# Interaction network on one core: VectorE splits x1 one group earlier and sums it one group later, and GpSimd issues four of quad 2's moves

## The chip, the core and the metric

One core of a Trainium2 chip runs the kernel. The metric is the device time of one execution in microseconds. The kernel before takes 678.15 us (median of 3 runs, 677.34 to 679.1).

## The reference

39 embedding rows of 16 numbers are looked up for each of 512 samples. Three interaction layers follow, each with 128 output maps, and a small dense network behind them:

```python
def _cin_layer(X0, Xi, W, b):
    Wr = W.reshape(H, F0_, Fi)
    return jnp.einsum('hjk,bjd,bkd->bhd', Wr, X0, Xi) + b[None, :, None]
# X0: 512 x 39 x 16 embeddings; Xi = X0, then the output of the layer before; H = 128
# every layer's output is summed over its 16 columns and kept
h = relu([sums of the 3 layers, dense_ctx] @ W_top1 + b_top1); h = relu(h @ W_top2 + b_top2); y = h @ W_top3
```

The output is one number for each sample.

## The kernel before

**Tiles and quads.** The 512 samples are cut into 64 tiles of 8 samples (128 columns: 8 samples times 16). Four tiles make a quad, so there are 16 quads, 0 to 15. T counts the tiles, ti = T % 4 is the tile's place in its quad.

**Layer 1** (the second of the three) is the bulk of the work and is done tile by tile. TensorE multiplies x1, the output of the first layer, with the weights in 10 groups g = 0 to 9 of four blocks of 128 columns (group 8 has three): `layer1`, lines 1151 to 1153, three matmuls a group, since x1 and the weights are each held as a high part and a low rest. The results lie in five banks of PSUM, group g in bank g % 5, so group g waits until the group five before it has been read. ScalarE reads groups 0, 1, 3, 4, 6, 7 and 9 (line 725), VectorE groups 2, 5 and 8 (lines 937 and 939). The text calls them VectorE's third, sixth and ninth group. GpSimd adds up pairs of what ScalarE made (`add_groups`, line 526, twice a tile; the second one waits for ScalarE's group 4). VectorE's `reduce_early` (line 947) stands between its groups 5 and 8 and waits for ScalarE's group 6 and for both additions of GpSimd, `reduce_late` (line 955) is done at the start of the next tile.

**Layer 0** makes x1 for the quad that comes next. For each quad GpSimd multiplies seven chunks (`multiply`, line 521; in quad 0 VectorE multiplies three quarters of them, `multiply_rest`, line 915), and TensorE sums them into one PSUM bank, `ps_x1` (`layer0`, line 1065; in quad 0 `sum_rest`, line 1136). The places of the chunks among the groups of layer 1 are written out by hand. While quad q >= 3 runs, chunk 0 of quad q + 1 is summed behind group 2 of the quad's first tile, and the last chunk, called LAST (number 6), behind group 2 of its fourth tile:

```python
SUMMED_AFTER = {(0, 2): 0, (0, 8): 1, (1, 1): 2, (1, 8): 3, (2, 5): 4, (3, 0): 5, (3, 2): LAST}
```

In quads 0 and 1 chunk 0 stands behind group 9 of the second tile, in quad 2 behind group 4 of the first. `ps_x1` is one bank, so chunk 0 has to wait until the x1 before it has been read from there:

```python
if c == 0:
    wait(pe, x1_lo_made, q)
    wait(pe, r1_made, q)
```

**Reading x1.** Three instructions read `ps_x1` in the fourth tile of a quad: ScalarE's `keep_x1` (line 653) makes the high part, VectorE's `split_x1` (line 855) the low rest, and waits for `keep_x1`; VectorE's `sum_x1` (line 860) sums over the 16 columns and signals `r1_made`. In quads 0 and 1 (`FREE_QUADS = 2`) the order on VectorE is: group 2, split, group 5, reduce_early, group 8, sum. In quads 2 to 14 it is: group 2, group 5, split, sum, reduce_early, group 8. ScalarE's `keep_x1` stands behind group 3 in quads 0 and 1 and behind group 4 later.

**Start of quad 0.** Tile 0 works on a quarter of x1 that is made ahead. The other three quarters are made during tile 0. VectorE's order is: group 2, chunks 3 and 4, group 5, chunks 5 and LAST, `spread` (line 848), reduce_early, `split_rest_x1` (line 920), sum_x1, group 8. TensorE sums chunks 5 and LAST behind group 7, then turns the rows of quad 1 (`turn_rows`, line 1028, waits for `spread`). Tile 1 waits for the low part.

**SyncE's queue and the last chunk.** SyncE issues the moves for each quad in a fixed order: shared rows (line 364), windows (line 387), the operands of the last chunk (`load_runs`, lines 374 and 375, four moves into `left` and four into `bz`, 20 KB each), and `lay_out` of the quad after (line 357, 32 moves in general, 16 in the part that is seen here). In quad 2 `load_runs` stands behind `lay_out(3)`. GpSimd gathers table rows (line 493) between its products. In tiles 4 to 7 it makes quad 2's chunks 0, 1, 2, gathers, chunks 3, 4, 5, two copies (lines 505 and 507), two gathers, and chunk LAST.

**Others.** Tiles 8 to 27 carry some extra work (the weights of layer 2 are turned): among the fourth tiles of quads, those of quads 2 to 6.

Of the kernel before, what the change touches and what calls it, by code (L numbers as in the profile page):

```python
# [35 lines left out]
RUN = 10  # L36
# [67 lines left out]
    return multiplied(q) if q == 3 else list(range(CHUNKS))  # L104


FIRST_SUMMED_AFTER = {2: [0], 3: [1], 4: [2], 5: [3], 6: [4], 7: [5, 6]}

SECOND_REGROUPED_AFTER = 3
NEXT_TURNED_AFTER, NEXT_KEPT_AFTER = [(0, 7), (0, 1)], [(0, 7), (0, 3)]  # L110
# [68 lines left out]
def build(nc, dense_ctx, ids, bases, table, W_top1, b_top1, W_top2, b_top2, W_top3, W0, b0, W1, b1, W2, b2, out):  # L179
# [8 lines left out]
    with ExitStack() as ctx:  # L188
# [117 lines left out]
        first_window = [None] + [sem(f"first_window_{c}") for c in range(1, LAST)]  # L306
        z_made, z_used = sem("z_made"), sem("z_used")
        runs_ld = [sem("runs_ld_0"), sem("runs_ld_1")]
        first_cut = [sem("first_cut_0"), sem("first_cut_1")]
        first_runs = sem("first_runs")  # L310
        z_hi_made, z_lo_made, z_stacked = sem("z_hi_made"), sem("z_lo_made"), sem("z_stacked")
# [37 lines left out]
        def _(sp):  # L349
# [16 lines left out]
            def load_runs(q, landed):  # L366

                if q - 1 >= STACKED_FROM:
                    sp.wait_ge(z_lo_made, q - STACKED_FROM)
                else:  # L370
                    sp.wait_ge(z_used, CHUNKS * (q - 1) + summed(q - 1).index(LAST) + 1)
                for n, (l, r) in enumerate(RUNS):
                    at = slice(RUN * n, RUN * (n + 1))
                    sp.dma_start(left[at, :], x0[l:l + RUN, q % 2, :]).then_inc(landed, 16)
                    sp.dma_start(bz[at, LAST, :], x0[r:r + RUN, q % 2, :]).then_inc(landed, 16)

            def stack(q):
# [99 lines left out]
        def _(pool):  # L477
# [31 lines left out]
            def multiply(q, c):  # L509
                if c == 0:  # L510
                    wait(pool, shared[q % 2], 16 * (SPC + 1) * ((q + 1) // 2))
                    wait(pool, z_used, CHUNKS * (q - 1) + 1)
                if c == 1:
                    wait(pool, first_cut[q % 2], 16 * len(window_parts(1)) * ((q + 1) // 2))
                if c == 2:
                    wait(pool, cut[q % 2], 16 * WINDOWS * ((q + 1) // 2))
                if c == LAST:
                    wait(pool, runs_ld[q % 2], 16 * 2 * len(RUNS) * ((q + 1) // 2))
                r = chunk_rows(c)
                window = bz[0:r, c, :] if c else x0[0:r, q % 2, :]  # L520
                nc.gpsimd.tensor_tensor(bz[0:r, c, :], window, left if c == LAST else xa[0:r, :], ALU.mult).then_inc(z_made, 1)  # L521
# [65 lines left out]
            multiply(2, 0)  # L587
            gather_behind(3, 9)
            multiply(2, 1)
            multiply(2, 2)  # L590
            make_index(4)
            for g in range(3):
# [37 lines left out]
        def _(act):  # L630
# [105 lines left out]
            for T in range(TILES):  # L736
# [3 lines left out]
                for g in ACT_GROUPS:  # L740
                    scale(T, g)
                    if (q, ti, g) == (1, 0, 4):
                        nc.scalar.copy(w0_stack[0:LEFT_ROWS, :], w0t[0:LEFT_ROWS, LAST, :]).then_inc(w0_hi_made, 1)
                    if STACKED_FROM <= q + 1 < QUADS and (ti, g) == SPLIT_LAST_AFTER:
                        split_last(q + 1)
                    if g == 6 and ti == 1 and q + 1 < QUADS:
                        keep_xt(q + 1)
                    if g == (3 if q < FREE_QUADS else 4) and ti == 3 and q + 1 < QUADS:
                        keep_x1(q + 1)
                    if (T, g) == (0, 7):  # L750
                        keep_rest_x1()
                    if (T, g) == (0, SECOND_REGROUPED_AFTER):
                        act.wait_ge(gathered[1], 16 * GATHERS)
                        for f in range(FPG // 2):
                            ins = regroup(nc.scalar.copy, 1, f)
                        ins.then_inc(regrouped_act, 1)
                    if q < FREE_QUADS and (ti, g) == NEXT_KEPT_AFTER[q]:
                        keep_x0(q + 1)
                    if FREE_QUADS - 1 <= q < QUADS - 2 and (ti, g) == (KEPT_AFTER if q >= FREE_QUADS else THIRD_KEPT_AFTER):
                        keep_x0(q + 2)  # L760
                    if g == 7 and T > 0:
                        keep_g(T - 1)
                    if g == 6 and T in W2_TURNED_IN:
                        n = W2_TURNED_IN[T]
                        act.wait_ge(w2_turned, n + 1)
                        nc.scalar.copy(w2_home(False, n).bitcast(F32R),
                                       ps_tr[:].rearrange("p (r c) -> p r c", c=HALF)).then_inc(w2_hi_made, 1)
# [20 lines left out]
        def _(dve):  # L788
# [173 lines left out]
            for T in range(TILES):  # L962
# [6 lines left out]
                if T == 0:  # L969
                    multiply_rest(3)  # L970
                    multiply_rest(4)
                if ti == 3 and q < FREE_QUADS:
                    split_x1(q + 1)
                scale_and_sum(T, DVE_GROUPS[1])
                if T == 0:
                    multiply_rest(5)
                    multiply_rest(6)
                    spread(0)
                if ti == 3 and FREE_QUADS <= q < QUADS - 1:
                    split_x1(q + 1)  # L980
                    sum_x1(q + 1)
                reduce_early(T)
                if T == 0:
                    split_rest_x1()
                    sum_x1(0)
                scale_and_sum(T, DVE_GROUPS[2])
                if ti == 3 and q < FREE_QUADS:
                    sum_x1(q + 1)
                if T == QT:
                    dve.wait_ge(w0_hi_made, 1)  # L990
# [276 lines left out]
```

## Time and profile before

| | |
|---|---|
| median of 3 runs | 678.15 us (677.34 to 679.1) |
| profiled execution | 677.4 us, span of the core 674.6 us |
| mean granted clock | 0.995 |
| TensorE busy | 653.3 us, 97% |
| ScalarE / VectorE / GpSimd busy | 572.2 / 517.9 / 455.4 us |

The profile follows one execution. The span runs from the first to the last instruction, and 2.8 us lie around it. TensorE is busy nearly all the time, so what matters is where TensorE waits. Its matmuls overlap, and the end of each is modelled: a stall is read from the distance between starts. In a stretch without a wait three matmuls of 512 columns start 0.23 to 0.24 us apart, and a group takes 0.70 us.

### The profile page before, as it was taken

Reading aid. Unit: us, or ns where it says so; the run is one execution under the profiler, and the core shown is the slowest. Engines: PE = TensorE matmul, PEld = TensorE weight load, DVE = VectorE, ACT = ScalarE, POOL = GpSimd, SP = SyncE. Lnnn points to the kernel's source line nnn. Section 1 sums busy time; section 2 is a strip of 40 time slices with the busy share of each in tenths; the row PEclk is TensorE's granted clock in tenths of the full one; section 3 lists DMA queues with packets and bytes.
Section 4 is the critical chain, followed back from the end, with each engine's and each line's share of the span. In section 5 each row is a group of like instructions: output and inputs, shape, how many; then the busy total and the mean of one; then the engine's idle time right before and its main releaser. Section 6 shows DMA issues by size and latency. Waiting matters only on the chain. (4 is left out here: it accounts for less than half of the span.)

```text
span 674.6 us, 10670 instructions
## 1 busy us (share of the span) xinstructions
PE 653.3 (97%) x2692; PEld 480.0 (71%) x2692; DVE 517.9 (77%) x1015; ACT 572.2 (85%) x2010; POOL 455.4 (68%) x443
## 2 busy tenths in 40 slices
PE   4889998999999999999999999999999999999998
PEld 4666766777777777777777777777777777776683
DVE  6578785678787878797878878788878797888780
ACT  3667976889898989898999989898989898999672
POOL 6748657777787878787887878787878655333000
PEclk9989998999999999999999999999999999999999
DMA  7222134223433425142421313131323121204300
GB/s 213 77 69 46 32 71 106 45 68 75 113 98 66 146 21 185 13 142 41 122 60 42 78 25 95 15 105 16 100 19 99 13 82 31 89 2 162 142 0 0
DMA packets 111155, 49.35 MB, mean 73 GB/s; under 512 B 82837, under 2 KB 95001, under 8 KB 111094
## 3 DMA queue, kind: packets, MB, share of 16 engines
q1 hardware_dynamic: 105120, 46.23, 26.1%
q0 software_dynamic: 5120, 1.29, 2.1%
q10 hardware_dynamic: 854, 1.16, 0.6%
q8 instruction: 21, 0.34, 0.2%
q14 instruction: 40, 0.33, 0.2%
HBM read 13.81 MB, written 5.24 MB: 28 GB/s over the span
## 5 line engine op out<-in xcount | busy, mean ns | idle before, releaser
L725 ACT ACTIVATE prod<-ps_y,xt 128x128 f32<-128x128 f32 x1792 | 494.7, 426 | 61.6 <-PE ps_y L1153 57.3
L1151 PE MATMUL ps_y<-w_hi,x_hi 128*128 128x512 f32 (+1 forms) x640 | 304.0, 475 | 2.3 <-issue 1.1
L1152 PE MATMUL ps_y<-w_lo,x_hi 128*128 128x512 f32 (+1 forms) x640 | 249.9, 391 | 0.0
L1153 PE MATMUL ps_y<-w_hi,x_lo 128*128 128x512 f32 (+1 forms) x640 | 249.9, 390 | 0.0
L526 POOL TENSOR_TENSOR prod<-prod 128x512 f32<-128x512 f32 x118 | 152.4, 1292 | 80.9 <-ACT prod L725 78.5
L939 DVE SCALAR_TENSOR_TENSOR prod<-ps_y,xt,prod 128x128 f32<-128x128 f32 x576 | 162.9, 341 | 30.4 <-PE ps_y L1153 30.1
L493 POOL DMA_INDIRECT rows<-in_table,index x160 | 155.2, 970 | 45.0 <-issue 31.2
L947 DVE TENSOR_REDUCE prod<-prod 128x128 f32<-128x1536 f32 (+1 forms) x64 | 117.5, 1835 | 57.3 <-ACT prod L725 43.3
L1151 PEld LDWEIGHTS ps_y<-w_hi,x_hi 128*128 128x128 f32 x640 | 120.8, 189 | 56.2 <-issue 20.5
L1152 PEld LDWEIGHTS ps_y<-w_lo,x_hi 128*128 128x128 f32 x640 | 121.2, 189 | 43.4 <-issue 20.4
L1153 PEld LDWEIGHTS ps_y<-w_hi,x_lo 128*128 128x128 f32 x640 | 121.0, 189 | 26.2
L521 POOL TENSOR_TENSOR room<-room 128x512 f32<-128x512 f32 (+2 forms) x90 | 115.8, 1294 | 7.7 <-DMA room<-room 7.5
L955 DVE TENSOR_REDUCE x<-prod 128x128 f32<-128x1536 f32 x64 | 111.8, 1747 | 6.0 <-ACT prod L725 2.7
L1065 PE MATMUL ps_x<-room,w0t 117*128 117x512 f32 (+5 forms) x186 | 96.1, 597 | 3.1 <-POOL room L521 3.1
L1168 PE MATMUL ps_g<-bd,x 128*128 128x320 f32 x128 | 45.4, 435 | 0.0
L1065 PEld LDWEIGHTS ps_x<-room,w0t 117*128 117x128 f32 (+5 forms) x186 | 33.9, 189 | 11.7 <-POOL room L521 5.2
L937 DVE TENSOR_SCALAR prod<-ps_y,xt 128x128 f32<-128x128 f32 x128 | 38.4, 341 | 0.7 <-PE ps_y L1153 0.6
L734 ACT COPY g_all<-ps_g 128x320 f32<-128x320 f32 x64 | 31.1, 485 | 3.4 <-PE ps_g L1168 3.4
L1168 PEld LDWEIGHTS ps_g<-bd,x 128*128 128x128 f32 x128 | 23.4, 190 | 7.6 <-DVE x L955 2.9
L773 ACT CAST g_hi<-g_all 128x512 fp32r<-128x512 f32 x39 | 23.9, 621 | 4.5 <-PE ps_y L1214 2.3
L505 POOL COPY emb_room<-emb_room 128x312 f32<-128x312 f32 x15 | 7.2, 477 | 24.9 <-DMA emb_room<-rows 24.9
L848 DVE TENSOR_TENSOR bd<-ps_tr,mask 128x1248 f32<-128x1248 f32 x16 | 23.1, 1443 | 0.0
(138 smaller groups left out, 367.1 us busy)
## 6 DMA issues: line engine op xcount, KB each, us to landing
room<-room SPq DMA_DIRECT2D x75, 234.0 KB
room<-room SPq DMA_DIRECT2D x45, 78.0 KB
emb_room<-rows SPq DMA_DIRECT2D x168, 5.0 KB
rows<-in_table,index POOLq DMA_INDIRECT x160
w_hi_dram<-g_all SPq DMA_DIRECT2D x5, 512.0 KB
w_lo_dram<-g_all SPq DMA_DIRECT2D x5, 512.0 KB
g_all<-in_L_rec_W SPq DMA_DIRECT2D x9, 256.0 KB, 6.1
g_all<-in_L_rec_W SPq DMA_DIRECT2D x4, 512.0 KB, 4.2
```

The lines of the kernel that those rows point to most:

```text
L493: pool.indirect_dma_start(out=rows[0:n, q % 2, g, :], out_offset=None, in_=table, in_offset=bass.IndirectOffsetOnAxis(ap=index[0:n, q % 2, ...
L521: nc.gpsimd.tensor_tensor(bz[0:r, c, :], window, left if c == LAST else xa[0:r, :], ALU.mult).then_inc(z_made, 1)
L526: nc.gpsimd.tensor_tensor(prod[:, SLOT[a]:SLOT[a] + 2], prod[:, SLOT[a]:SLOT[a] + 2], prod[:, SLOT[b]:SLOT[b] + 2], ALU.add).then_inc(pool ...
L725: ins = nc.scalar.activation(prod[:, SLOT[k] + m // 2, :, m % 2], ps_y[:, g % YBANKS, m * H:(m + 1) * H], ACT.Copy, scale=xt[:, q % 2, ti, ...
L939: ins = nc.vector.scalar_tensor_tensor(out=a, in0=y, scalar=x, in1=a, op0=ALU.mult, op1=ALU.add)
L947: nc.vector.tensor_reduce(prod[:, BIASED, :, 0], prod[:, EARLY if adds(T) else EARLY_FIRST].rearrange("p n h l -> p h n l"), AX_XY, ALU.ad ...
L955: nc.vector.tensor_reduce(x2[:, T % 2, :], prod[:, LATE[T % 2]].rearrange("p n h l -> p h n l"), AX_XY, ALU.add).then_inc(reduced, 1)
L1065: nc.tensor.matmul(ps_x1[:], w, z, start=c == 0, stop=c == summed(q)[-1]).then_inc(z_used, 1)
L1151: nc.tensor.matmul(y, hi, w1_hi[:, cols], start=True, stop=False)
L1152: nc.tensor.matmul(y, hi, w1_lo[:, cols], start=False, stop=False)
L1153: nc.tensor.matmul(y, lo, w1_hi[:, cols], start=False, stop=True).then_inc(y_made, 1)
L1168: nc.tensor.matmul(ps_g[:, 0:(F + 1) * TB], x2[:, T % 2, :], bd[:, T // QT % 2, T % QT].rearrange("p j b -> p (j b)"), start=True, stop=Tr ...
```

## The change

In every quad that makes a next x1 (0 to 14) VectorE's order in the fourth tile becomes: group 2, split_x1, group 5, reduce_early, group 8, sum_x1. ScalarE's `keep_x1` stands behind group 3 in all of them. In tile 0 the last chunk is multiplied behind reduce_early, x1 is split and summed behind group 8, TensorE sums the last chunk behind group 9 and ScalarE makes the high part behind its group 9. SyncE no longer issues the four moves into `left` for quad 2. GpSimd issues them behind chunk 1 of quad 2, and its last product of quad 2 waits for them by a semaphore of their own.

```diff
-FIRST_SUMMED_AFTER = {2: [0], 3: [1], 4: [2], 5: [3], 6: [4], 7: [5, 6]}
+FIRST_SUMMED_AFTER = {2: [0], 3: [1], 4: [2], 5: [3], 6: [4], 7: [5], 9: [LAST]}
...
+        left_ld = sem("left_ld")
...
-                    sp.dma_start(left[at, :], x0[l:l + RUN, q % 2, :]).then_inc(landed, 16)
+                    if q != 2:
+                        sp.dma_start(left[at, :], x0[l:l + RUN, q % 2, :]).then_inc(landed, 16)
                     sp.dma_start(bz[at, LAST, :], x0[r:r + RUN, q % 2, :]).then_inc(landed, 16)
...
                 if c == LAST:
-                    wait(pool, runs_ld[q % 2], 16 * 2 * len(RUNS) * ((q + 1) // 2))
+                    if q == 2:
+                        pool.wait_ge(left_ld, 16 * len(RUNS))
+
+                    wait(pool, runs_ld[q % 2], 16 * len(RUNS) * (2 * ((q + 1) // 2) - (q % 2 == 0)))
...
             multiply(2, 1)
+
+            pool.wait_ge(x0_made, 3)
+            pool.wait_ge(z_made, CHUNKS * 2)
+            for n, (l, r) in enumerate(RUNS):
+                pool.dma_start(left[RUN * n:RUN * (n + 1), :], x0[l:l + RUN, 0, :]).then_inc(left_ld, 16)
             multiply(2, 2)
...
-                    if g == (3 if q < FREE_QUADS else 4) and ti == 3 and q + 1 < QUADS:
+                    if g == 3 and ti == 3 and q + 1 < QUADS:
                         keep_x1(q + 1)
-                    if (T, g) == (0, 7):
+                    if (T, g) == (0, 9):
                         keep_rest_x1()
...
-                if ti == 3 and q < FREE_QUADS:
+                if ti == 3 and q + 1 < QUADS:
                     split_x1(q + 1)
                 scale_and_sum(T, DVE_GROUPS[1])
                 if T == 0:
                     multiply_rest(5)
-                    multiply_rest(6)
                     spread(0)
-                if ti == 3 and FREE_QUADS <= q < QUADS - 1:
-                    split_x1(q + 1)
-                    sum_x1(q + 1)
                 reduce_early(T)
+                if T == 0:
+                    multiply_rest(LAST)
+                scale_and_sum(T, DVE_GROUPS[2])
                 if T == 0:
                     split_rest_x1()
                     sum_x1(0)
-                scale_and_sum(T, DVE_GROUPS[2])
-                if ti == 3 and q < FREE_QUADS:
+                if ti == 3 and q + 1 < QUADS:
                     sum_x1(q + 1)
```

## Rows read from the trace of the kernel before

**Rows 1.** Page, part 1: busy us, share of the span, instructions.
```profile
PE 653.3 (97%) x2692; PEld 480.0 (71%) x2692; DVE 517.9 (77%) x1015; ACT 572.2 (85%) x2010; POOL 455.4 (68%) x443
```

**Rows 2.** Waits of PE: who, for whom, us in total, times, longest.
```profile
PE ps_x L1065 <- POOL room L521: 3.1, 4, 2.2
```

**Rows 3.** Timeline of PE, tile 7: start, us, instruction, count, idle before.
```profile
108.96 1.12 PE L1065 MATMUL ps_x<-room,w0t 40*128 40x512 f32 x2 [2.18 <-POOL room L521]
```

**Rows 4.** Timeline of GpSimd and of SyncE's queue, tiles 5 to 7.
```profile
85.93 1.32 POOL L521 TENSOR_TENSOR room<-room 127x512 f32<-127x512 f32 x1
93.52 1.29 POOL L521 TENSOR_TENSOR room<-room 126x512 f32<-126x512 f32 x1 [6.27 <-DMA room<-room]
107.65 1.25 POOL L521 TENSOR_TENSOR room<-room,g_hi 40x512 f32<-40x512 f32 x1 [2.22 <-DMA room<-room]
...
100.00 0.82 SPq L374 DMA_DIRECT2D g_hi<-room  x1
105.48 0.72 SPq L375 DMA_DIRECT2D room<-room  x1
```

**Rows 5.** Page, part 5, GpSimd's gathers: count, busy us, mean ns, idle before.
```profile
L493 POOL DMA_INDIRECT rows<-in_table,index x160 | 155.2, 970 | 45.0 <-issue 31.2
```

**Rows 6.** Stretches: width, PE, PEld, DVE, ACT, POOL busy (count), PE clock, DMA, GB/s.
```profile
39.50:42.90 3.40, 2.90 (x10) 2.55 (x10) 3.40 (x3) 1.16 (x2) 0.57 (x1) 0.50 0.00 0
111.20:114.60 3.40, 3.40 (x10) 2.61 (x9) 1.76 (x5) 2.65 (x9) 3.01 (x4) 0.50 0.42 125
114.70:118.00 3.30, 3.30 (x16) 2.72 (x15) 2.17 (x3) 3.12 (x12) 2.98 (x4) 1.00 0.53 168
```

**Rows 7.** Timeline of PE and of DVE, tile 0.
```profile
38.54 0.91 PE L1136 MATMUL ps_x<-room,w0t 40*128 40x384 f32 x2 [1.66 <-DVE room L915]
43.16 0.50 PE L1151 MATMUL ps_y<-w_hi,x_hi 128*128 128x512 f32 x1
...
37.94 0.55 DVE L915 TENSOR_TENSOR room<-room,g_hi 40x384 f32<-40x384 f32 x1 [2.78 <-DMA room<-room]
38.41 1.44 DVE L848 TENSOR_TENSOR bd<-ps_tr,mask 128x1248 f32<-128x1248 f32 x1
39.78 2.80 DVE L947 TENSOR_REDUCE prod<-prod 128x128 f32<-128x2560 f32 x1
42.51 0.60 DVE L920 SCALAR_TENSOR_TENSOR x_lo<-ps_x,columns,x_hi 128x384 fp32r<-128x384 f32 x1
```

**Rows 8.** Timeline of ACT, tile 0.
```profile
39.49 0.58 ACT L708 ACTIVATE x_hi<-ps_x,columns 128x384 fp32r<-128x384 f32 x1 [2.07 <-PE ps_x L1136]
```

**Rows 9.** Timeline of PE, DVE, ACT, POOL, tile 47 into 48.
```profile
484.05 1.02 PE L1065 MATMUL ps_x<-room,w0t 128*128 128x512 f32 x2
...
481.11 0.68 DVE L860 TENSOR_REDUCE r<-ps_x 128x32 f32<-128x512 f32 x1
481.70 1.74 DVE L947 TENSOR_REDUCE prod<-prod 128x128 f32<-128x1536 f32 x1
483.37 0.86 DVE L939 SCALAR_TENSOR_TENSOR prod<-ps_y,xt,prod 128x128 f32<-128x128 f32 x3
...
479.66 0.74 ACT L653 ACTIVATE x_hi<-ps_x,columns 128x512 fp32r<-128x512 f32 x1
...
480.11 1.31 POOL L526 TENSOR_TENSOR prod<-prod 128x512 f32<-128x512 f32 x1
```

**Rows 10.** The same places, tile 19 into 20: PE, then DVE.
```profile
230.27 1.02 PE L1065 MATMUL ps_x<-room,w0t 128*128 128x512 f32 x2
...
229.18 0.86 DVE L939 SCALAR_TENSOR_TENSOR prod<-ps_y,xt,prod 128x128 f32<-128x128 f32 x3
```

**Rows 11.** The same places, tile 43 into 44: PE, then POOL.
```profile
447.73 1.02 PE L1065 MATMUL ps_x<-room,w0t 128*128 128x512 f32 x2
448.90 0.50 PE L1151 MATMUL ps_y<-w_hi,x_hi 128*128 128x512 f32 x1 [0.15 <-DVE prod L939]
...
444.91 1.32 POOL L526 TENSOR_TENSOR prod<-prod 128x512 f32<-128x512 f32 x1
```

## The prediction, written before the changed kernel ran

> **What bounds the kernel now.** I read the page's part 1 first: PE is busy 97% of the span, the next engine 85% [rows 1]. TensorE is the bound, and a gain or a loss has to show as a wait of TensorE or as a change of its clock. So the second view is the list of PE's waits. Only two entries of it belong to the change: the sums of layer 0 waiting for GpSimd's products, 3.1 us in all, of which one wait is 2.2 us [rows 2], and the sum in tile 0 waiting for VectorE, 1.7 us [rows 7]. The third view is the timeline at these two places, the fourth the granted clock of stretches around them, and the last the timelines of all engines at the end of a quad, since the change reorders work there in every quad.
>
> **Quad 2's last chunk.** TensorE stands 2.18 us in tile 7 until GpSimd has multiplied the last chunk [rows 3]. GpSimd itself stood 2.22 us before this product, from 105.43 to 107.65, for the moves of the operands [rows 4]. SyncE issued those eight moves one after another, from 100.00 to 106.20, so 0.78 us each, and the data were there 1.45 us after the last issue [rows 4]. With four of them gone the last of SyncE's four is issued at about 103.1 and has landed at about 104.6, before GpSimd is ready at 105.43. The product then ends at 106.7 and not at 108.9. TensorE is ready for the chunk at about 106.6, so nearly all of its wait goes: 2.1 us.
>
> The four moves that GpSimd takes over stand behind chunk 1's product, which ends at 87.25, and GpSimd then stands until 93.52 for the windows [rows 4]. A direct move issued by GpSimd isn't in the trace. Its nearest row is an indirect one of GpSimd, 0.97 us on average [rows 5]; from below the nearest is SyncE's 0.72 us [rows 4]. Four cost 2.9 to 3.9 us and up to 5 us with the gaps between gathers, and the idle stretch of 6.27 us covers all of it. If that cover were gone, chunks 2 to LAST would be late by the whole of it. The two waits put ahead of them (x0_made, z_made) are for things that earlier instructions of GpSimd already needed: nothing. The four moves run beside the window moves that end that idle stretch. Each carries 10 rows, a window 117 to 127, and there are eight window moves; I take 0.1 us, between 0 and 0.4.
>
> The Trainium skill, page "DMA: Bandwidth & Descriptors", section "Issuing engines are not separate DMA queues", speaks against this part: moves from any engine run on the same 16 DMA engines, and a second issuer saves only the sequencer's time, "which is usually small relative to the DMA itself". Here the trace differs: the sequencer's 6.2 us stand against 1.45 us from the last issue to the data [rows 4]. By the page's rule this part would bring nothing; that is the third rival below.
>
> **The clock behind it.** From 111.2 to 114.6 the granted clock is 0.50, that is 1.2 GHz, right behind this wait, and TensorE starts 10 matmuls there, against 16 in the next 3.3 us at full clock [rows 6]. The lost part is half of 3.4 us, 1.7 us. The only other stretch at 0.50 within these tiles follows the other long wait, in tile 0 [rows 6, 7]. With the wait gone I expect the second drop to go as well: 1.7 us. TensorE then reaches tile 8's group 3 earlier than GpSimd's additions and VectorE's group 8 of tile 7 allow, by about 0.4 us, since GpSimd gains only 2.2 us. Sum for quad 2: 2.1 + 1.7 - 0.4 + 0.1 of cost = 3.3 gained, bounds 1.6 (the drop stays) to 3.9.
>
> **Tile 0.** Now VectorE waits 2.78 us for the last chunk's operands, from 35.16 on, and spread (1.44) and reduce_early (2.80) stand behind it [rows 7]. In the new order spread runs at once and ends at 36.5, reduce_early ends at 39.3, the last product (0.55) at 39.75. TensorE meanwhile turns the rows and does groups 8 and 9, which end at about 38.8; at present they come only behind the last chunk. It sums the last chunk at 39.8, that is 1.2 us later than now (38.54). ScalarE starts the high part 0.95 us after that sum's start [rows 7, 8]: 40.75, done at 41.33; VectorE has done group 8 by then and splits until 41.95 (0.60). Tile 1 starts at about 42.0 and not at 43.16 [rows 7]: 1.1 us gained. sum_x1, 0.68 us behind it, is next needed a tile later: nothing.
> **The clock in tile 1** counts against this. Now the drop from 39.5 on [rows 6] costs next to nothing, as tile 1 has to wait for the split at 43.11 anyhow. In the new order TensorE waits 1.0 us and then 1.4 us within 3.3 us, and a drop that follows falls on tile 1, where TensorE has no wait: 1.7 us. I take it that it comes. Tile 0: +0.6 us, bounds -1.1 and +0.7.
>
> **The end of every quad from 2 on.** This decides. In tile 47 the present order is split, sum_x1 481.11 (0.68), reduce_early 481.70 (1.74), group 8 from 483.37 to 484.23, and TensorE starts chunk 0 of the quad after next at 484.05 [rows 9]. That chunk waits for `r1_made`, which sum_x1 signals, and this was done at 481.79: a margin of 2.3 us. In the new order sum_x1 stands behind group 8. It can't end before about 484.8, and the chunk waits for it, at the head of TensorE's queue, with group 3 of the next tile and all behind it.
>
> Does reduce_early come earlier, now that split and sum no longer stand right before it? It waits for ScalarE's group 6, which is not moved by the swap (keep_x1 and group 4 change places), and for GpSimd's second addition, which waits for group 4. ScalarE's keep_x1 takes 0.57 us of its time (0.74 [rows 9], of which the next instruction overlaps some 0.17), so group 4 is later by that: it ends at about 480.4 and not at 479.8, the addition runs from 480.5 to 481.8 and not from 480.11 [rows 9]. reduce_early starts at about 481.88, 0.2 us later than now. Group 8 ends at 484.4, sum_x1 at 485.0, chunk 0 starts at 485.05: TensorE loses 1.0 us.
> - Seven quad ends are of this kind (tiles 31, 35, ... 55). In five of them, as tile 43, GpSimd is late: its second addition starts 2.8 us ahead of TensorE's chunk 0 (444.91, 447.73) where in tile 47 it is 3.9 us, and group 3 of the next tile already waits for VectorE's group 8, starting 1.17 us behind chunk 0 and not some 0.46 [rows 9, 11]. If GpSimd stays late the loss there is 1.05 us. If a longer quad lets it catch up (its lateness comes from waiting for the lay_out moves), it is 0.5 us in the three latest and 0.9 us in the others. I take that it catches up: 3 x 0.5 + 2 x 0.9 + 2 x 1.0 = 5.3.
> - Five quad ends (tiles 11, 15, 19, 23, 27) have a turn of four blocks behind group 4, so TensorE comes to chunk 0 later against VectorE: at 230.27, 0.23 behind the end of group 8, and not 0.18 ahead of it [rows 9, 10]. 5 x 0.58 = 2.9.
>
> Sum 8.2 us. From above, with GpSimd as late as now, 10.6. From below, if GpSimd's addition never held reduce_early, so that ScalarE's group 6 set it: 3.9. I take 8.2, as group 4 and the addition behind it are rows with little play. The earlier split brings nothing: TensorE has no wait on x_lo after tile 1. Group 5 comes 1.1 us later at most, and its bank is next needed 0.7 us behind its new end, in a tile of the first kind. The last two quad ends make no chunk 0 behind them or stand in quads 0 and 1, where the order is already the new one.
>
> **Sum.** 677.4 - 3.3 + 0.6 + 8.2 = 682.9 us for the profiled execution. That execution is 0.75 us under the median of the three runs, so the same sum gives 683.6 at the median. I predict 683.3.
>
> **The rivals.**
> - *The clock drops at the quad ends too.* A wait of 1 us is new in 12 places. For it: both long waits of the trace are followed by 0.50 [rows 6]. Against: those were 1.7 and 2.2 us long, and two stretches of 3.4 us at 0.50 are all that the mean clock of 0.995 leaves room for, so no shorter wait brought one. Each drop costs 1.7 us; four of them give 690, all twelve 704. The Trainium skill ("TensorE: Matmul & The Clock Gate", section "HAM oscillation") tells of a loop where this comes back at "every single K-tile". Chance 0.12.
> - *Faster: VectorE is done in time.* If sum_x1 ended before TensorE comes to chunk 0, only the gains at quads 0 and 2 would stay: 678.15 - 3.3 - 1.1 = 673.7. It decides at a loss of 0.37 us a quad end, under which the gains outweigh it; VectorE's group 8 would have to end some 0.4 us earlier than now. For it: VectorE is idle 23% of the span [rows 1]. Against: of the two releases of reduce_early one doesn't move and one moves later. With the lower bound of 3.9 and no drop in tile 1 the time is 677.7. Chance of this side 0.08.
> - *Quad 2's chunk comes no earlier.* GpSimd's own moves land late or cost more than the idle stretch, and the wait of 2.2 us and the drop stay: 683.3 + 3.3 = 686.6. Chance 0.15.
> - *The chunk 0 wait is there, but the net is nothing* (loss near its lower end, both gains full): 678. Chance 0.05.
>
> The forecast has 0.60. Its own range is 680.5 to 686. The whole range, 679 to 689, takes in the third rival and a few clock drops. A difference of 0.3% is 2.0 us, about what a measurement can tell here. Faster 0.08 is the second rival; same 0.08 is the fourth and 0.03 from the forecast's lower edge; the rest, 0.84, is slower.
>
> **What would show it.** In the changed profile: PE's waits list gets an entry of layer 0 (now line 1065) released by VectorE's sum_x1, 12 times, around 0.6 to 1.0 us each. GpSimd's last product of quad 2 starts within 0.1 us of its gather's end, and PE's wait for it is under 0.3 us. Four moves on GpSimd's queue lie in the stretch where it waited 6.27 us. Tile 1 starts about 1 us earlier. Quads 8 to 14 last about 0.8 us longer each. The prediction is wrong if TensorE starts chunk 0 where it does now, or if the granted clock shows more than two stretches at 0.50.

## The result and the profile after

The changed kernel takes 683.45 us (median of 6 runs, 682.24 to 687.47) against 678.19 us for the kernel before (6 runs on the same chip): the ratio is 1.0085, interval 1.0063 to 1.0107. The profiled execution took 685.1 us, span 683.0 us. The forecast, 683.3 us, and its sign came out. That the number is so near is in part luck: in the profiled execution the term for tile 0 was 2.1 us too high and the one for the quad ends 2.0 us too low, and the two errors cancelled.

First the page of after, part 1 (busy us, share, instructions):

```profile
PE 653.3 (96%) x2692; PEld 478.7 (70%) x2692; DVE 519.0 (76%) x1015; ACT 573.5 (84%) x2010; POOL 458.1 (67%) x447
```

Beside [rows 1] no engine has more work to speak of; GpSimd has four instructions more. TensorE's 653.3 us are the same, so the 8.3 us by which the span grew are waits. The waits of PE (for whom, who ended them, us in total, times, longest):

```profile
PE ps_x L1073 <- issue: 8.8, 12, 1.0
PE ps_y L1159 <- DVE x_lo L930: 1.3, 1, 1.3
PE ps_y L1159 <- DVE prod L949: 1.2, 4, 0.5
PE ps_x L1144 <- DVE room L925: 1.1, 1, 1.1
PE ps_x L1073 <- POOL room L526: 0.5, 2, 0.3
```

Line 1073 is `layer0`, 1065 before. The first entry is new: 12 waits, 8.8 us. The list counts 8.8 us, where the starts of the matmuls give a loss of 10.2 us (the table below): a wait in the list begins only at the modelled end of the matmul before it. The fifth entry is what is left of [rows 2], where it was 3.1 us. The second and fourth are tile 0. The third stood at 1.0 us in 4 waits before.

**Where the time went.** I took the distance from the first matmul of each tile to that of the next in both profiled executions, and summed it by quad:

| stretch | after minus before, us | forecast |
|---|---|---|
| start of the span to tile 0 | +2.93 | 0 |
| quad 0 (all of it in tile 0: 16.36 to 14.84) | -1.52 | +0.6 |
| quad 1 (tile 7: 13.36 to 9.64) | -3.84 | -3.7 |
| quad 2 (tile 8: 9.96 to 10.48) | +0.52 | +0.4 |
| quads 3 to 14: .75 .71 .72 .71 .77 1.14 .91 1.00 .83 .98 .59 1.13 | +10.24 | +8.2 |
| quad 15 | -0.02 | 0 |
| sum | +8.3 | +5.5 |

**The quad end.** Timelines of PE, ACT, DVE and POOL in tile 47 and the start of 48 (start, us, instruction, idle before). This execution is later as a whole: TensorE starts group 3 of tile 47 at 482.33 here and at 476.69 in before, and times are compared counted from there:

```profile
490.75 1.10 PE L1073 MATMUL ps_x<-room,w0t 128*128 128x512 f32 x2 [0.89 <-issue]
491.28 0.79 PE L1159 MATMUL ps_y<-w_hi,x_hi 128*128 128x512 f32 x1
...
484.31 0.71 ACT L663 ACTIVATE x_hi<-ps_x,columns 128x512 fp32r<-128x512 f32 x1
...
485.05 0.75 DVE L865 SCALAR_TENSOR_TENSOR x_lo<-ps_x,columns,x_hi 128x512 fp32r<-128x512 f32 x1 [1.04 <-ACT x_hi L663]
487.52 1.75 DVE L957 TENSOR_REDUCE prod<-prod 128x128 f32<-128x1536 f32 x1 [0.69 <-ACT prod L735]
489.19 0.86 DVE L949 SCALAR_TENSOR_TENSOR prod<-ps_y,xt,prod 128x128 f32<-128x128 f32 x3
489.96 0.68 DVE L870 TENSOR_REDUCE r<-ps_x 128x32 f32<-128x512 f32 x1
...
486.13 1.30 POOL L531 TENSOR_TENSOR prod<-prod 128x512 f32<-128x512 f32 x1 [0.40 <-ACT prod L735]
```

`sum_x1` (line 870) runs from 489.96 to 490.64, and chunk 0 starts at 490.75, 0.1 us behind its end. Before, the same sum ended at 481.79 and the chunk started at 484.05 [rows 9]: a margin of 2.3 us has become a wait of 0.89. VectorE works through reduce_early, group 8 and the sum without a gap, and was idle 0.69 and 1.04 us just before. The list of waits names the releaser "issue" and not the sum; that it is the sum is read from the 0.1 us between the two, which is the same at all twelve quad ends (tiles 11, 15, ... 55), and shown by the experiments.

**Quad 2's last chunk.** Tile 7: PE, then POOL, then SyncE's queue.

```profile
107.69 0.39 PE L1161 MATMUL ps_y<-w_hi,x_lo 128*128 128x512 f32 x1
108.11 1.12 PE L1073 MATMUL ps_x<-room,w0t 40*128 40x512 f32 x2
...
88.58 2.14 POOL L599 DMA_DIRECT2D g_hi<-room  x4
94.37 1.30 POOL L526 TENSOR_TENSOR room<-room 126x512 f32<-126x512 f32 x1 [3.65 <-DMA room<-room]
106.74 1.31 POOL L526 TENSOR_TENSOR room<-room,g_hi 40x512 f32<-40x512 f32 x1
...
102.01 3.17 SPq L377 DMA_DIRECT2D room<-room  x4
```

The 2.22 us of GpSimd and the 2.18 us of TensorE [rows 3, 4] are gone. SyncE issues four moves (102.01 to 105.18) and not eight. GpSimd's four took 2.14 us, 0.54 each, inside the stretch in which it had waited 6.27 us.

**The clock and tile 0.** Stretches (width, PE, PEld, DVE, ACT, POOL busy, clock, DMA, GB/s), then PE and DVE of tile 0:

```profile
112.00:116.00 4.00, 4.00 (x19) 3.26 (x19) 3.31 (x6) 4.00 (x17) 3.64 (x4) 1.00 0.44 139
27.00:44.00 17.00, 14.33 (x66) 10.22 (x65) 11.56 (x25) 11.49 (x42) 9.52 (x18) 1.00 0.27 76
```
```profile
42.34 0.91 PE L1144 MATMUL ps_x<-room,w0t 40*128 40x384 f32 x2 [1.13 <-DVE room L925]
44.57 0.50 PE L1159 MATMUL ps_y<-w_hi,x_hi 128*128 128x512 f32 x1 [1.32 <-DVE x_lo L930]
...
37.65 1.45 DVE L858 TENSOR_TENSOR bd<-ps_tr,mask 128x1248 f32<-128x1248 f32 x1
39.02 2.81 DVE L957 TENSOR_REDUCE prod<-prod 128x128 f32<-128x2560 f32 x1
41.74 0.54 DVE L925 TENSOR_TENSOR room<-room,g_hi 40x384 f32<-40x384 f32 x1
43.90 0.62 DVE L930 SCALAR_TENSOR_TENSOR x_lo<-ps_x,columns,x_hi 128x384 fp32r<-128x384 f32 x1 [0.84 <-ACT x_hi L718]
```

Both stretches at half clock of [rows 6] are gone. The order in tile 0 is the forecast one, with waits of 1.13 and 1.32 us, and here no drop followed them.

### The profile page after: what moved, and what is told of

It is laid out like the page before. It is cut to its first block and busy times, and to the rows that moved or that the text cites. A ratio compares the mean times of both kernels' runs of the same rounds, so it can differ in the third digit from the quotient of the medians.

```text
span 683.0 us, 10672 instructions
## 1 busy us (share of the span) xinstructions
PE 653.3 (96%) x2692; PEld 478.7 (70%) x2692; DVE 519.0 (76%) x1015; ACT 573.5 (84%) x2010; POOL 458.1 (67%) x447
## 5 line engine op out<-in xcount | busy, mean ns | idle before, releaser
L495 POOL DMA_INDIRECT rows<-in_table,index x160 | 157.4, 984 | 43.8 <-issue 28.5
L865 DVE SCALAR_TENSOR_TENSOR x_lo<-ps_x,columns,x_hi 128x512 fp32r<-128x512 f32 x15 | 11.3, 751 | 18.7 <-ACT x_hi L663 16.6
```

The costliest lines, as they stand in the source:

```text
L495: pool.indirect_dma_start(out=rows[0:n, q % 2, g, :], out_offset=None, in_=table, in_offset=bass.IndirectOffsetOnAxis(ap=index[0:n, q % 2, ...
```

## The experiments

The chips of the three batches differ: the kernel before has a median of 683.4, 683.6 and 677.9 us on them, and the profiled executions differ mostly in the stretch ahead of tile 0 (the kernel with GpSimd's moves alone starts tile 0 at 33.3 us on the second chip and at 26.3 us on the third). Ratios are therefore each to the kernel before on the same chip, and where a run is said to be some us longer or shorter, that is its ratio times this median, unless medians are named. An expected time is compared by its ratio to 678.2 us. "Quads 3 to 14" is the sum of the table above, against the profiled execution of before.

### What in the quad end costs the time

Only the sum goes back ahead of reduce_early; the early split and keep_x1 stay:

```diff
+                if ti == 3 and FREE_QUADS <= q < QUADS - 1:
+                    sum_x1(q + 1)
                 reduce_early(T)
 ...
-                if ti == 3 and q + 1 < QUADS:
+                if ti == 3 and q < FREE_QUADS:
                     sum_x1(q + 1)
```

> The changed kernel, with sum_x1 put back ahead of reduce_early from quad 2 on; the earlier split and ScalarE's earlier keep_x1 stay. Theory (the sum behind group 8 holds TensorE's chunk 0 of the next quad, 12 times some 0.85 us, 10.2 us in all in the profile after): the waits for sum_x1 go and the time falls from 683.4 to about 673. Rival 1 (the swap of keep_x1 and group 4, which makes GpSimd's second addition and reduce_early 0.2 us later, costs a good part): it stays above 676. Rival 2 (the earlier split itself brings something): it comes out more than 1 us under the kernel with the whole quad end undone.

Measured: 682.3 us, ratio 0.997 (0.9941 to 0.9999). The waits of chunk 0 are gone; quads 3 to 14 take 1.7 us more than before, mostly in small stalls of tiles 31 to 43, where after has 10.2. The time is not the expected one: 673 us would be a ratio of 0.992.

The whole quad end of before put back into after:

```diff
-                    if g == 3 and ti == 3 and q + 1 < QUADS:
+                    if g == (3 if q < FREE_QUADS else 4) and ti == 3 and q + 1 < QUADS:
 ...
+                if ti == 3 and FREE_QUADS <= q < QUADS - 1:
+                    split_x1(q + 1)
+                    sum_x1(q + 1)
                 reduce_early(T)
 ...
```

> The changed kernel with the whole quad end as before from quad 2 on (group 5, split, sum, reduce_early, group 8; keep_x1 behind ScalarE's group 4); the parts in tile 0 and at quad 2's last chunk stay. Theory: these two parts alone bring 1.1 to 1.5 us and 3.8 us less 0.4 us, against the kernel before: 673.0 to 674.0. If they bring nothing in the median, 678.

Measured: 682.9 us, ratio 0.9973 (0.9937 to 1.0009); quads 3 to 14 +1.3, with one stall of 1.5 in tile 35. The two kernels differ by 0.6 us, well inside either interval: that split and keep_x1 stand earlier is worth nothing that shows in the medians. What costs is where the sum stands. This run too is short of its expectation, 0.992 to 0.994, which was for the two other parts alone. As the quad ends of the two kernels differ and their times do not, the shortfall lies outside the quad ends; the new order in tile 0 turns out below to be worth less than the expectation took.

The stall in tile 35 is a wait for the low part, which the list of TensorE's waits of this run shows so:

```profile
PE ps_y L1162 <- DVE x_lo L865: 1.3, 1, 1.3
```

VectorE had stood for 2.42 us ahead of its group 5, and so ahead of the split. The profile names TensorE as what it waited for, but by their records the matmuls of that group end 2.6 us before VectorE reads them. The ends are modelled, so a late end and a late signal can't be told apart. Such a wait for the split of a quad end stands in four of the eight profiled executions with the split behind group 5 (0.6, 0.6, 1.3 and, in four waits, 2.9 us) and in none of the six with the split ahead of it. So the earlier split may guard TensorE when VectorE's group 5 is late. No run tests that by itself.

The release later, or its user later? Chunk 0 is summed behind group 4 and not behind group 2:

```diff
-SUMMED_AFTER = {(0, 2): 0, (0, 8): 1, (1, 1): 2, (1, 8): 3, (2, 5): 4, (3, 0): 5, (3, 2): LAST}
+SUMMED_AFTER = {(0, 4): 0, (0, 8): 1, (1, 1): 2, (1, 8): 3, (2, 5): 4, (3, 0): 5, (3, 2): LAST}
```

> The changed kernel, all parts kept, but chunk 0 of the next quad is summed behind group 4 and not group 2 of a quad's first tile, from quad 3 on. Theory (TensorE waits at chunk 0 for the sum alone): chunk 0 then comes 1.4 us later, 0.8 us behind the end of sum_x1, no wait is left and the time is 673 to 674. Rival (VectorE's queue as a whole is late at this place, so that the wait moves to groups 3 or 7): above 677.

Measured: 684.2 us, ratio 1.0017 (0.999 to 1.0044), where 0.993 was expected of a chunk that waits for nothing and the kernel with the sum back reached 0.997. Waits of PE and the same place in tile 48:

```profile
PE ps_y L1159 <- DVE prod L949: 3.3, 11, 0.5
...
491.13 0.50 PE L1159 MATMUL ps_y<-w_hi,x_hi 128*128 128x512 f32 x1 [0.25 <-DVE prod L949]
492.64 1.02 PE L1073 MATMUL ps_x<-room,w0t 128*128 128x512 f32 x2
```

The wait for the sum is gone. In its place group 3 of the next tile waits for VectorE's group 8, whose bank it takes: that group ends 7.72 us behind the start of TensorE's group 3, and group 3 of the next tile starts at 7.77. The waits are 3.3 us in the list (1.0 us of them, 4 times, stood there before too), and quads 3 to 14 take 3.4 us more than before, a third of after's loss. In before, chunk 0 stands at this place and is 0.46 us of work that covers the same group 8 (7.53 there). The chunk can't leave its place for nothing.

The margin tested from the other side, by a second sum in each quad end:

```diff
                     sum_x1(q + 1)
+                    if q >= FREE_QUADS:
+                        nc.vector.tensor_reduce(r1[:, QB * (q + 1):QB * (q + 2)].rearrange("p (t b) -> p t b", b=TB),
+                                                ps_x1[:].rearrange("p (t d b) -> p t b d", d=D, b=TB), AX_X,
+                                                ALU.add).then_inc(summed_once, 1)
+                        dve.wait_ge(summed_once, q - 1)
```

> The changed kernel, with the sum over x1's columns done twice in a row at each quad end from quad 2 on (the same numbers are written twice). One more sum costs VectorE 0.68 us and a short wait for the first. Theory (sum_x1 stands on TensorE's path at 12 quad ends): 12 times 0.65 to 0.75 us are added, 691 to 693. Rival (there is play behind it): under 687.

Measured: 701.7 us, ratio 1.0248 (1.0193 to 1.0303).

```profile
PE ps_x L1079 <- issue: 18.0, 12, 1.9
165.04 2.04 PE L1079 MATMUL ps_x<-room,w0t 128*128 128x512 f32 x2 [1.85 <-issue]
```

The same 12 waits are 18.0 us, 0.77 longer each; each of quads 4 to 14 takes 0.62 to 0.76 more than in after, and quads 3 to 14 together 11.3 more. The second sum is paid in full: in after there is no slack left at this place. Tile 12 alone takes 13.55 us and not 10.9 as its like in the other quads. Its wait, the second line, is the longest of the twelve, and the granted clock is at half from 164.9 to 168.3, from about the end of this wait. The other eleven, of 1.2 to 1.6 us, have no half clock behind them. By the ratios this kernel is 11.1 us over after, where 7.6 to 9.6 was expected; 2.6 us of it is what tile 12 has over its like.

### The parts alone

Only the quad ends, put into before (three places: keep_x1 behind group 3, split behind group 2, sum behind group 8):

> The kernel before with the new quad ends alone (split ahead of group 5, sum behind group 8, keep_x1 behind group 3, from quad 2 on). Theory: 12 waits of chunk 0, 10 us more than the 678.2 of the kernel before, 687.5 to 689. Rival (the parts add up otherwise, GpSimd stays late without the others): 690.

Measured: 694.7 us, ratio 1.0174 (1.0126 to 1.0222), that is +11.9 us.

```profile
PE ps_x L1062 <- issue: 9.4, 12, 1.1
PE ps_x L1062 <- POOL room L521: 3.3, 2, 3.1
```

The first line is the loss (11.2 us over quads 3 to 14); the second holds the wait for quad 2's last chunk, which this kernel keeps; it was 2.2 us in before. Its quads 4 to 14 are those of after within 0.05 us each; the first, quad 3, has 1.75 where after has 0.75. The ratio is that of the rival (690 us), but its reason is not borne out: GpSimd catches up as in after. VectorE at the quad end ahead of it:

```profile
157.73 0.75 DVE L855 SCALAR_TENSOR_TENSOR x_lo<-ps_x,columns,x_hi 128x512 fp32r<-128x512 f32 x1 [2.46 <-ACT x_hi L653]
```

In after the same wait is 1.43 us. The extra 1.0 us begins on ScalarE: it reads group 3 of tile 11 from 2.40 us behind TensorE's start of that group, and in after from 1.35, though the records of the matmuls stand alike. The run with the sum twice has the same delay at the same place. Its cause stays open, as in tile 35 above.

Only GpSimd's four moves, put into before:

```diff
-                    sp.dma_start(left[at, :], x0[l:l + RUN, q % 2, :]).then_inc(landed, 16)
+                    if q != 2:
+                        sp.dma_start(left[at, :], x0[l:l + RUN, q % 2, :]).then_inc(landed, 16)
 ...
+            for n, (l, r) in enumerate(RUNS):
+                pool.dma_start(left[RUN * n:RUN * (n + 1), :], x0[l:l + RUN, 0, :]).then_inc(left_ld, 16)
```

> The kernel before with GpSimd issuing quad 2's four moves into left, and nothing else. Theory (SyncE's queue of issues is what makes the last chunk late): GpSimd's last product of quad 2 starts right behind its gathers, TensorE's wait of 2.2 us goes and the stretch at half clock with it: 678.2 - 3.4 = 674.8. If the half clock comes all the same: 676.3. Rival (the DMA engines are the limit, whoever issues): 678.

Measured: 680.3 us, ratio 0.9949 (0.9922 to 0.9976), that is -3.5 us, as expected (0.995); tile 7 takes 9.64 us.

```profile
92.22 2.15 POOL L599 DMA_DIRECT2D g_hi<-room  x4
98.59 1.30 POOL L526 TENSOR_TENSOR room<-room 126x512 f32<-126x512 f32 x1 [4.22 <-DMA room<-room]
110.63 1.30 POOL L526 TENSOR_TENSOR room<-room,g_hi 40x512 f32<-40x512 f32 x1
```

Is it GpSimd as a second issuer, or that the four moves go out early? Before, with the four moves issued by SyncE ahead of lay_out(3):

```diff
+                if q == 2:
+                    for n, (l, r) in enumerate(RUNS):
+                        sp.dma_start(left[RUN * n:RUN * (n + 1), :], x0[l:l + RUN, 0, :]).then_inc(runs_ld[0], 16)
```

> The kernel before with the same four moves into left still issued by SyncE, but ahead of lay_out(3) and not behind it. Theory (SyncE's issues follow one another without a gap from 78.8 to 106.2 us, so only a second issuer helps): lay_out is 2.9 us later, the four moves into bz still end at 106, GpSimd's last product starts at about 107.6 as now, and the time stays within 0.5 us of 678.2. Rival (what helps is that fewer moves stand behind lay_out, whoever issues them): 674.8 as with GpSimd.

Measured: 682.3 us, ratio 0.9987 (0.9957 to 1.0018): no gain to be told. SyncE's queue, GpSimd, and the waits of PE:

```profile
92.48 3.02 SPq L439 DMA_DIRECT2D g_hi<-room  x4
95.61 10.57 SPq L357 DMA_DIRECT2D emb_room<-rows  x16
106.23 3.15 SPq L376 DMA_DIRECT2D room<-room  x4
...
107.52 0.44 POOL L509 COPY emb_room<-emb_room 128x312 f32<-128x312 f32 x1 [1.81 <-DMA emb_room<-rows]
110.94 1.28 POOL L525 TENSOR_TENSOR room<-room,g_hi 40x512 f32<-40x512 f32 x1 [0.40 <-DMA room<-room]
...
PE ps_tr L1032 <- POOL emb_room L511: 2.2, 1, 2.2
```

The four moves cost SyncE 3.02 us here too, as half of its eight did in before (3.1 of 6.2). Put ahead, they push lay_out back by as much, GpSimd's copy stands 1.81 us for it, and TensorE's 2.2 us stand at turn_rows. Tile 7 is shorter (13.36 to 10.00), with no half clock left in it, and tile 6 longer (13.31 to 14.85). That is 1.8 us gained over both, where GpSimd's moves gain 3.6. So in the trace the rival has half of the gain, and the second issuer the other half. The profiled execution gives it back in quads 3 to 14 (+3.6 us, 2.9 of it in four waits for the low part, told of above), and the median can't tell 1.8 us from none.

Only tile 0's new order, put into before (last chunk behind reduce_early, split behind group 8, summed behind TensorE's group 9):

> The kernel before with the new order in tile 0 alone (last chunk multiplied behind reduce_early, x1 split and summed behind group 8, the last chunk summed behind group 9). Theory A (the two waits of about 1 us do not bring the half clock into tile 1): 1.1 to 1.5 us faster, 676.7 to 677.1. Theory B, the prediction's (half clock falls on tile 1): 0.6 us slower, 678.8.

Measured: 686.0 us, ratio 1.0041 (1.0008 to 1.0074), that is +2.8 us, more than either theory had. Tile 0 takes 14.83 us (16.36 before), tile 1 10.38 us (9.0 in after). Stretches around it:

```profile
45.50:48.90 3.40, 1.27 (x4) 0.29 (x2) 2.56 (x6) 1.73 (x5) 0.87 (x1) 1.00 0.12 25
49.00:52.40 3.40, 3.17 (x8) 2.50 (x9) 2.44 (x3) 1.29 (x5) 0.94 (x1) 0.50 0.36 113
52.50:55.90 3.40, 3.40 (x18) 2.53 (x17) 1.30 (x5) 2.99 (x12) 1.88 (x2) 1.00 0.52 160
```

That is the drop on tile 1 of the forecast: 8 matmuls at 1.2 GHz where the next stretch has 18, behind a stretch in which TensorE was busy 1.27 of 3.40 us. It is not the whole difference. In tile 7 GpSimd waits longer than in before for the last chunk's operands, and TensorE with it:

```profile
115.90 1.25 POOL L521 TENSOR_TENSOR room<-room,g_hi 40x512 f32<-40x512 f32 x1 [3.08 <-DMA room<-room]
```

TensorE stands 3.04 us and not 2.18 there, the half clock behind it lasts 6.8 us and not 3.4, and tile 7 takes 15.79 us for 13.36. The kernel with the quad ends alone, on the same chip, has the longer wait too. The kernel before was not profiled on this chip, so whether the chip or the change makes it longer stays open, and with it how much of the 2.8 us is tile 0's.

### All parts on one chip, and two versions

Four kernels beside 23 runs of before (677.9 us). After itself again:

> The changed kernel itself, beside the next three on one chip, since the chips of the runs so far differ by some 5 us in the time of the kernel before. Theory: it stands to the kernel before as the sum of its parts, the quad ends some 10 us, the moves -3.5 us, tile 0 between -1.5 and +2.8 us: 1.008 to 1.014.

Measured: 684.1 us, ratio 1.0083 (1.0065 to 1.01); quads 3 to 14 +10.2. With the quad end of before, as above:

> The changed kernel with the quad ends as before, on the same chip as the changed kernel. Theory (12 waits of chunk 0 for sum_x1, 0.6 to 1.1 us each): 9 to 10.5 us under the changed kernel, and, as tile 0's new order gains nothing when the prologue is slow, 0 to 3 us under the kernel before.

Measured: 674.3 us, ratio 0.9955 (0.9934 to 0.9976); quads 3 to 14 -0.03, and of the waits of layer 0 only this one is left:

```profile
PE ps_x L1076 <- POOL room L526: 0.8, 2, 0.6
```

The quad end is the one difference between these two kernels, and it is 9.8 us between the medians, 8.7 us by the ratios, 10.2 us over quads 3 to 14 of the traces. GpSimd's moves without the rest:

> The kernel before with GpSimd's four moves alone, on the same chip as the others. Theory: 3.5 us faster than before, 0.995, and faster than every kernel that has the new quad ends or the new tile 0.

Measured: 673.6 us, ratio 0.9943 (0.9924 to 0.9962). And a middle way for tile 0: spread ahead of the last chunk's product, which stays ahead of reduce_early and is summed behind group 8, with the split, the sum and ScalarE's high part of tile 0 where they were, and the quad end of before (against after):

```diff
 ...
                     multiply_rest(5)
                     spread(0)
+                    multiply_rest(LAST)
+                if ti == 3 and FREE_QUADS <= q < QUADS - 1:
+                    split_x1(q + 1)
+                    sum_x1(q + 1)
                 reduce_early(T)
 ...
```

> The kernel before with GpSimd's four moves and a smaller step in tile 0: spread is put ahead of the last chunk's product and TensorE sums the last chunk behind group 8; reduce_early, split and sum stay where they were. VectorE then fills its wait for the operands with spread (1.44 us), and TensorE fills its own with the turn and group 8. Theory (the new order of tile 0 costs since the product stands behind the 2.8 us of reduce_early): tile 0 gets 0.5 to 1.4 us shorter than in the kernel with the moves alone, which is 1.005 times faster than before; this one 0.992 to 0.994. Rival (tile 0 is bound by reduce_early and the split in any order): the same as with the moves alone, 0.995.

Measured: 673.0 us, ratio 0.9936 (0.9914 to 0.9959), the fastest of all, but only 0.5 us under the moves alone; that is not told apart. Its tile 0 takes 14.29 us against 16.60, and its tile 1 10.36 against 9.02, as a half clock now falls on tile 1. VectorE, and then PE's first matmul behind the wait for the low part, there:

```profile
35.98 1.45 DVE L858 TENSOR_TENSOR bd<-ps_tr,mask 128x1248 f32<-128x1248 f32 x1
38.48 0.55 DVE L925 TENSOR_TENSOR room<-room,g_hi 40x384 f32<-40x384 f32 x1 [1.05 <-DMA room<-room]
...
42.34 0.80 PE L1161 MATMUL ps_y<-w_hi,x_hi 128*128 128x512 f32 x1 [1.45 <-DVE x_lo L930]
```

From before to after on this chip, by medians, the steps are: moves -4.3 (677.9 to 673.6), tile 0 +0.7 (to 674.3, inside the noise), quad ends +9.8 (to 684.1). Such steps make +6.2 by construction. Whether the parts add up is told by the runs with each part alone, and they don't quite: +11.9, -3.5 and +2.8 make +11.2, and after stands at +5.6 by its ratio. The intervals, taken together, leave room for some 4.5 us of this difference. The parts were measured on another chip than the whole, and the rest stays open.

## Why the prediction was right, and where it was not

**Quad 2's last chunk: right.** Forecast 3.3 gained, the trace shows 3.32 (quads 1 and 2 together), the runs of this part alone 3.5 and 3.9 by the ratios. The wait, the drop behind it and GpSimd's lag of 0.4 to 0.5 us in tile 8 came as worked out. The cost of GpSimd's moves was taken too high: 2.9 to 3.9 us from the gathers [rows 5], measured 2.14. As the idle stretch covered them either way, nothing followed. The Trainium skill ("DMA: Bandwidth & Descriptors", section "Issuing engines are not separate DMA queues") says that a second issuer saves only the sequencer's time, and that this is usually small. The second half does not hold here. The moved issues were 3.0 to 3.2 us of a queue that was itself the bound, and SyncE issuing them earlier moved 2.2 us of waiting to turn_rows.

**The quad ends: the mechanism right, the size 2.0 us too small.** Of the steps for tile 47, seen from TensorE's group 3 of that tile, the addition of GpSimd (forecast 3.8, measured 3.80), reduce_early (5.19), group 8's end (7.72) and the sum's end (8.31) are all within 0.05 us of the forecast, and chunk 0 starts at 8.42 for 8.35 (8.41 to 8.43 in ten of the twelve, 8.56 in tile 43 and 8.82 in tile 11, where GpSimd's addition is later). That GpSimd catches up was right in four of the five late quad ends; in tile 43 it is still 0.13 us late. The terms that were mis-sized are two. In the clean case I had group 3 start at 8.81, and it starts at 8.95 (7.82 before): the chunk comes 0.07 later and the group 0.53 and not 0.46 behind it, and this is paid in all 12 quads. In the late case I took the loss from the starts of group 3, where it had already waited for group 8 [rows 11]. But that wait had been partly free: when group 3 starts on time, group 4 follows 1.11 us behind (tile 48, 7.82 and 8.93), as the rest of the chunk's work lies between; when it starts late, 0.80 us behind (tile 44, 8.64 and 9.44). A wait ahead of the chunk is paid in full. In after the first tile of quads 8 to 14 takes 10.2 to 10.3 us whatever it took before (9.08 to 9.53). The run with the sum back shows what the sum's place is worth alone: 8.5 of the 10.2 us. Two slips of the recorded text belong here. Its bound from above, 10.6, comes to 10.15 by its own terms (5 x 1.05 + 2 x 1.0 + 2.9). And its sum gives 683.6 at the median, which it lowers to 683.3 without a reason.

**Tile 0: not one number.** In the trace of after the part gained 1.5 us, and no drop fell on tile 1. Of the eight profiled executions with the new order four had a half clock in tile 1 (10.4 to 10.5 us) and four did not; of five with the old order none had it there. So the forecast drop is real and comes in half of the executions; I had taken it as certain. The gain of 1.1 us is not a constant either: with the old order tile 0 is as long as the last chunk's operands take to land. Counted from the start of tile 0 the product begins at 11.14 us in before, 11.38 in one run of the moves alone, 9.73 in the other, 9.26 with the quad ends alone and 8.23 with SyncE's moves ahead, and tile 0 takes 16.36, 16.60, 14.96, 14.49 and 13.45 us. VectorE in tile 0 of the 16.60 us one, and of the 13.45 us one:

```profile
37.71 0.55 DVE L925 TENSOR_TENSOR room<-room,g_hi 40x384 f32<-40x384 f32 x1 [3.03 <-DMA room<-room]
```
```profile
41.48 0.55 DVE L919 TENSOR_TENSOR room<-room,g_hi 40x384 f32<-40x384 f32 x1 [0.22 <-DMA room<-room]
```

The new order puts the product behind reduce_early, at 12.0 us or later, so it never takes less than 14.83, and took 16.4 in the five executions in which a half clock fell into it, 15.74 in one without. Where the operands land late it can win 1.5 us; where they land early it loses. The forecast worked from one execution in which they landed late [rows 7]. The step that failed is that one landing time was taken for all. Tile 0 cost 0.7 us between the medians of the moves alone and the same with the new order, which their intervals don't tell from nothing, and 2.8 us put alone into before, on another chip and with a longer wait in tile 7; the forecast was +0.6.

**Outside the sum** stand the 2.9 us by which the profiled execution of after came later to tile 0, with the same instructions as before there. That execution is 2.2 us over the forecast 682.9: +2.9 there, +2.0 at the quad ends, -2.1 in tile 0, and 0.6 less outside the span. The median is within 0.2 us of 683.3.

**The rivals.** The clock did not drop at the quad ends: after's span has one stretch at half clock, at 22.5 to 25.9, ahead of tile 0. That VectorE is in time is refuted by the 12 waits; that the chunk comes no earlier, by tile 7; that the net is nothing, by 10.2 us lost at the quad ends against 4.8 gained in quads 0 to 2. The sign by which that wait was to be known failed, though the wait came: the forecast wait would be listed as released by VectorE; it is listed as "issue".

**What stays open:** why the stretch ahead of tile 0 lasts 26 to 30 us in the executions of the result and of the last batch and 33 to 35 in the others; what decides whether a half clock follows in tile 1; why VectorE and ScalarE read a group 1 to 2.6 us late at a few quad ends; whether the earlier split guards TensorE then; why the wait in tile 7 is 3.0 us and not 2.2 in two kernels on the second chip; and whether spread ahead of the product is worth its 0.5 us.

## What to carry to other kernels

An instruction that frees a buffer is placed by when its user needs the buffer, not by when the instruction's own input is ready: here a sum of 0.68 us with 2.3 us of margin was put behind 2.6 us of other work, and 12 times TensorE paid up to 1.0 us. When a wait is removed by moving its user, look at what is next late on the same engine. Where one queue issues small moves at 0.8 us each and the data are there 1.5 us after the last, a second issuer helps; another order in the same queue brought half as much in the trace, because it made others in the queue wait, and nothing to be told in the median. And the parts of a change are best measured as steps on one chip: alone, on another one, they made 11.2 us where the whole was 5.6.

## What the runs showed of the hardware

- A direct move of 10 rows of 2 KB took GpSimd 0.54 us to issue, an indirect one 0.97 [rows 5], one of SyncE 0.72 to 0.82 [rows 4].
- A fall of TensorE's clock to 1.2 GHz is not the same from one execution to the next: behind waits of 1.1 and 1.3 us in tile 0 it came in four of eight. The twelve waits at the quad ends of after, five of 0.45 to 0.56 us and seven of 0.9 to 1.0, brought none; with the sum done twice they were 1.2 to 1.9 us, and it came behind the longest alone.
- The kernel before ran 0.8% slower on two chips than on the third. No profile of it was taken there. The kernel with GpSimd's moves alone, profiled on one of the two and on the third, has spans of 678.6 and 671.4 us, and starts tile 0 at 33.3 and 26.3 us.
- At a few quad ends VectorE or ScalarE read a group of TensorE's late against the records of its matmuls: ScalarE 1.0 us later than in after (tile 11, in two executions), VectorE 2.6 us behind the modelled end (tile 35, in one). Where the split or the sum stood behind that read, TensorE paid 1.0 to 1.5 us for it.
